# One block for the network and the second attention: the first sequence goes ahead beside the second sequence's down projection

## The reference

```python
x = x + _L0_attn_ref(_layernorm(x), wq, wk, wv, wo)            # 32 heads of 128, 8 key/value heads
x = x + _L0_ffn_ref(_layernorm(x), gate_t, up_t, down_t, ...)  # 512 -> 1792 -> 512, ternary weights with scales
x = x + _L1_attn_ref(_layernorm(x), w_qkv, b_qkv, w_out, b_out)# 32 heads of 16, ALiBi, causal
x = x + _L1_ffn_ref(_layernorm(x), A, B, Wr)                   # 64 experts, 16 picked
```

## Time and profile before

| what | value |
|---|---|
| median of 3 runs | 1610.68 us |
| the profiled execution's own time | 1609.08 us |
| its span | 1607.2 us |
| mean granted TensorE clock | 0.968 of full |
| share of the span: PE / DVE / ACT / POOL | 91 / 63 / 53 / 33 % |

### The profile page before, as it was taken

The page is one execution under the profiler, slowest core; times in us unless marked ns, Lnnn a source line. Parts: engine busy times, 40 slices in busy tenths (PEclk is TensorE's granted clock), DMA queues, the critical chain, the costliest instruction groups (busy, mean ns, idle before and its releaser), DMA issues. The chain is left out here.

```text
span 1607.2 us, 25387 instructions
## 1 busy us (share of the span) xinstructions
PE 1469.5 (91%) x7696; PEld 1208.1 (75%) x7696; DVE 1013.9 (63%) x2543; ACT 857.9 (53%) x2181; POOL 534.8 (33%) x465
## 2 busy tenths in 40 slices
PE   5999999999999999999778999995879999986798
PEld 3778888888888888888666888873667777764587
DVE  6676767676666676666544333344768888897543
ACT  2666555665566565556514233202768888894210
POOL 3673555545456554462400000005331313110500
PEclk9999999999999999999998999997889999997899
DMA  4010010101001010000002111005333444422000
GB/s 147 20 47 14 27 40 20 39 13 33 26 26 33 13 33 26 26 7 8 20 6 100 59 59 59 0 0 129 74 73 83 86 78 90 74 42 98 17 21 27
DMA packets 37468, 71.97 MB, mean 45 GB/s; under 512 B 4976, under 2 KB 5360, under 8 KB 36848
## 3 DMA queue, kind: packets, MB, share of 16 engines
q1 hardware_dynamic: 29664, 55.35, 11.3%
q0 software_dynamic: 7728, 15.73, 6.0%
HBM read 60.58 MB, written 10.49 MB: 44 GB/s over the span
## 5 line engine op out<-in xcount | busy, mean ns | idle before, releaser
L728 ACT ACTIVATE a_probs<-a_probs,a_least 128x512 f32<-128x512 f32 (+3 forms) x256 | 142.9, 559 | 175.6 <-DVE a_least L629 168.3
L377 POOL TENSOR_TENSOR a_rotated<-a_by_cos,a_by_sin 128x512 f32<-128x512 f32 x80 | 103.4, 1292 | 248.3 <-DVE a_by_sin L652 246.2
L637 DVE TENSOR_TENSOR a_probsT_lo<-a_ps_turn,a_probsT_hi 128x512 fp32r<-128x512 f32 (+3 forms) x256 | 118.7, 485 | 71.2 <-ACT a_probsT_hi L736 69.7
L736 ACT CAST a_probsT_hi<-a_ps_turn 128x512 fp32r<-128x512 f32 (+3 forms) x256 | 101.3, 426 | 102.0 <-PE a_ps_turn L526 102.0
L1532 ACT ACTIVATE a_probs<-a_probs,a_least 128x128 f32<-128x128 f32 (+3 forms) x256 | 142.3, 561 | 12.5 <-DVE a_least L1435 9.7
L1435 DVE CUSTOM_DVE_ANT_0 a_probs<-a_ps_score,a_causal 128x128 f32<-128x128 f32 (+3 forms) x256 | 117.2, 486 | 40.8 <-PE a_ps_score L1323 31.0
L782 ACT ACTIVATE a_probs<-a_probs,a_inverse 128x128 f32<-128x128 f32 (+3 forms) x256 | 123.2, 553 | 8.7 <-DVE a_inverse L690 7.5
L64 PE MATMUL a_ps_out<-a_wo_hi,a_attended_hi 128*128 128x512 f32 x256 | 105.5, 412 | 17.8 <-POOL a_wo_lo L371 15.6
L629 DVE CUSTOM_DVE_ANT_0 a_probs<-a_ps_score,a_causal 128x512 f32<-128x512 f32 (+2 forms) x192 | 101.1, 551 | 28.8 <-PE a_ps_score L66 28.7
L387 POOL TENSOR_TENSOR a_query_lo<-a_rotated,a_query_hi 128x512 fp32r<-128x512 f32 x64 | 82.6, 1290 | 105.8 <-ACT a_query_hi L748 105.8
L1443 DVE TENSOR_TENSOR a_probsT_lo<-a_ps_turn,a_probsT_hi 128x384 fp32r<-128x384 f32 (+1 forms) x192 | 108.9, 595 | 2.7 <-ACT a_probsT_hi L1541 2.6
(11 more groups left out here) (250 smaller groups left out, 4205.6 us busy)
## 6 DMA issues: line engine op xcount, KB each, us to landing
a_raw<-in_wq SPq DMA_DIRECT2D x36, 256.0 KB, 2.6
a_raw<-in_wo SPq DMA_DIRECT2D x36, 256.0 KB, 2.7
a_stacked_q<-a_spill_q POOLq DMA_DIRECT2D x48, 128.0 KB, 5.0
a_stacked_k<-a_spill_k POOLq DMA_DIRECT2D x24, 256.0 KB, 4.6
f_raw<-in_gate SPq DMA_DIRECT2D x14, 256.0 KB, 2.8
f_raw<-in_up SPq DMA_DIRECT2D x14, 256.0 KB, 3.0
f_raw<-in_down SPq DMA_DIRECT2D x14, 256.0 KB, 3.5
a_raw<-in_wk SPq DMA_DIRECT2D x12, 256.0 KB, 2.7
```

Of the source, the lines that this page charges most:

```text
L377: nc.gpsimd.tensor_tensor(rotated[:], by_cos[:], by_sin[:], ALU.add).then_inc(rotation_added, 1)
L637: nc.vector.tensor_tensor(probsT[1][:, t % 2, 0:w], ps_turn[:, t % 2, 0:w], probsT[0][:, t % 2, 0:w].bitcast(F32), ALU.subtract).then_inc( ...
L728: nc.scalar.activation(tile, tile, ACT.Exp, bias=least[:, slot, i:i + 1], scale=-1.0, accum_out=total[:, slot, i:i + 1]).then_inc(exp_done, 1)
L736: nc.scalar.copy(probsT[0][:, t % 2, 0:w], ps_turn[:, t % 2, 0:w]).then_inc(turned_hi, 1)
```

## The change

Both phases become one function with one block (`ffn0_attention1_phase`); the network is a class `Ffn0` whose parts are called by the engines' streams of the joint block. All its tiles and those of the attention lie at fixed places in one piece of SBUF and share the space as it comes free: `stacked_q` of a sequence lies on down-projection chunks 0 to 1 (2 to 3), `stacked_k` on 4 (5). PE tells of freed chunks by `chunk_free`.

The layer norm of the third layer has two parts of four tiles each, with the steps as methods. The PSUM banks are shared: the second sequence's down projection now goes to the four banks of gate and up, not to those of the first sequence.

```diff
@@ LayerNorm
+    def tiles(self, part): ...     # the tiles of one of `parts` parts
+    def shift / invert / normalise / split / root / round / turn / ready (…, part or tile)
@@ network, down projection of the second sequence
-            for t in range(QT):
-                at = slice(t * P, (t + 1) * P)
-                pe.wait_ge(out_scaled, t + 1)
-                for f in range(FC):
-                    mm = product(nc, ps_out[:, t, :], ...
+    def second_sequence(self, pe, t, chunks):
+        for f in chunks:
+            mm = product(nc, self.out_bank(t), ...
+            if f == FC - 1: mm.then_inc(self.out_done, 1)
+            elif t == NT - 1: mm.then_inc(self.chunk_free, 1)
@@ block.tensor
-            norm.tensor(pe)
-            pe.wait_ge(pick_in, 16)
+            ffn.tensor(pe)
+            ffn.second_sequence(pe, 4, range(FC))
+            ffn.second_sequence(pe, 5, range(half))
+            norm.turn(pe, 0)
+            ffn.second_sequence(pe, 5, range(half, FC))
+            norm.ready(pe, 0)
+            side_work(-1, 7)
+            ffn.second_sequence(pe, 6, range(half))
+            side_work(-1, 8)
+            ffn.second_sequence(pe, 7, range(half))
+            ffn.second_sequence(pe, 6, range(half, FC))
+            ffn.second_sequence(pe, 7, range(half, FC))
+            side_work(-1, 9)
...
+            pe.wait_ge(pick_in[0], 16)
+            pe.wait_ge(ffn.out_scaled, 6)
+            step(-1, 13)
+            side_work(-1, 10)
+            norm.turn(pe, 1)
+            pe.wait_ge(pick_in[1], 16)
             each_chunk(pe, step)      # now starts at step (-1, 14)
@@ block.vector
-            norm.vector(dve)
-            dve.wait_ge(consts_in, 16 * 3)
+            ffn.vector(dve)
+            for t in range(QT): ffn.add_out(dve, t)
+            norm.shift(dve, 0); norm.invert(dve, 0); normalise and split tiles 0 to 3
+            norm.normal_free(dve, 0)
+            ffn.add_out(dve, 4); ffn.add_out(dve, 5)
+            dve.wait_ge(bias_in, 16)
+            step(-1, 8); step(-1, 9)
+            ffn.add_out(dve, 6); ffn.add_out(dve, 7)
+            norm.shift(dve, 1)
+            dve.wait_ge(causal_in, 16)
+            step(-1, 13)
+            norm.invert(dve, 1); normalise tiles 4 to 7
+            step(-1, 11)
+            split tiles 4 to 7; norm.normal_free(dve, 1)
@@ block.scalar
-            norm.scalar(act)
+            ffn.scalar(act); norm.root(act, 0); norm.round(act, 0)
+            step(-1, 8); step(-1, 9); norm.root(act, 1)
+            step(-1, 10); step(-1, 11); norm.round(act, 1)
@@ block.sync
+            ffn.sync(sp)
+            sp.dma_start(bias[:], dram["bias1"]).then_inc(bias_in, 16)
+            sp.wait_ge(ffn.weights_split, 3 * FC)
             (wq, wk, wv, causal, wo)
+            write_out(-1, 7)
+            write_out(-1, 8)
+            sp.wait_ge(ffn.chunk_free, 8)
+            (out_bias)
+            write_out(-1, 15)
@@ block.gpsimd
+            def prepare(b):
+                pool.wait_ge(ffn.chunk_free, 2 * b + 2)
+                (half of `pick` for sequence b; clear stacked_q of b)
+            pool.wait_ge(ffn.made, 2 * FC)
             for what in ("wq", "wk", "wv"): split(1, ...)
-            (clear stacked_q) ; read_back(-1, 7), (-1, 8), (-1, 15) ; add the output bias ; chunk(0)
+            prepare(0)
+            read_back(pool, -1, 7)
+            pool.wait_ge(ffn.chunk_free, 5)
+            read_back(pool, -1, 8)
+            prepare(1)
+            read_back(pool, -1, 15)
+            chunk(0): read_back(pool, 0, 0), then add_out_bias(), then the split of wq
```

More of the change, by code:

```diff
@@ L141, in tensor, with turn @@
+    def scalar(self, act):
+        self.root(act, 0)
+        self.round(act, 0)
+    def turn(self, pe, part):
         nc, m, tiles_before = self.nc, self.m, self.tiles_before
@@ L144, in tensor @@
             pe.wait_ge(m.ident_in, 16)
-        for t in range(NT):
+        for t in self.tiles(part):
             pe.wait_ge(normal_done, tiles_before + t + 1)
@@ L839, in ffn0_phase @@
[L839 to L855, removed]
-                    sp.dma_start(raw[:, k, w, :], dram[name][f]).then_inc(raw_in[k][w], 16)
-            fetch(0, 0)
-            fetch(1, 1)
-            with sp.Fori(1, FC // 2) as i:
-                for k in range(2):
-                    fetch(2 * i + k, k)
@@ new lines, in scalar, with vector, copy_columns, split_lo @@
+        self.norm.scalar(act)
+        split_hi(0, 0, 1)
+        chunk(0, 0, 1)
+        chunk(1, 1, 1)
+        with act.Fori(1, FC // 2 - 1) as i:
+            for k in range(2):
+                chunk(2 * i + k, k, i + 1)
+        chunk(FC - 2, 0, FC // 2)
+        chunk(FC - 1, 1, FC // 2, last=True)
+    def vector(self, dve):
+        nc, gate, up, down = self.nc, self.gate, self.up, self.down
+        def copy_columns(f, k):
+            if isinstance(f, int) and f == 0:
+                dve.wait_ge(self.scales_in, 48)
+            wait(dve, self.hidden_made, 2 * f - 2)
+            nc.vector.tensor_copy(self.gate_col[:, k:k + 1], self.gate_s[:, bass.ds(f, 1)])
+            nc.vector.tensor_copy(self.up_col[:, k:k + 1], self.up_s[:, bass.ds(f, 1)]).then_inc(self.columns_copied, 1)
+        def split_lo(f, k):
@@ new lines, in add_to_sums @@
+                if last:
+                    mm.then_inc(self.out_done, 1)
+                elif t == QT - 1:
+                    mm.then_inc(self.summed, 1)
+        self.norm.tensor(pe)
+        make(0, 0, 0)
+        make(0, 0, 1)
+        make(1, 1, 0)
+        add_to_sums(0, 0, first=True)
+        make(1, 1, 1)
+        with pe.Fori(1, FC // 2) as i:
+            for k in range(2):
+                make(2 * i + k, k, 0)
+                add_to_sums(2 * i + k - 1, 1 - k)
+                make(2 * i + k, k, 1)
@@ L1405, in _ @@
         def _(dve):
-            norm.vector(dve)
-            dve.wait_ge(consts_in, 16 * 3)
+            ffn.vector(dve)
+            for t in range(QT):
+                ffn.add_out(dve, t)
+            norm.shift(dve, 0)
+            norm.invert(dve, 0)
+            for t in range(QT):
+                norm.normalise(dve, t)
+            for t in range(QT):
+                norm.split(dve, t)
+            norm.normal_free(dve, 0)
+            ffn.add_out(dve, 4)
+            ffn.add_out(dve, 5)
+            dve.wait_ge(bias_in, 16)
             def add_bias(c, s):
@@ L1517, in step @@
                     split_turned(*turning, 2)
+            step(-1, 8)
+            step(-1, 9)
+            ffn.add_out(dve, 6)
+            ffn.add_out(dve, 7)
+            norm.shift(dve, 1)
+            dve.wait_ge(causal_in, 16)
+            step(-1, 13)
+            norm.invert(dve, 1)
+            for t in range(QT, NT):
+                norm.normalise(dve, t)
+            step(-1, 11)
+            for t in range(QT, NT):
+                norm.split(dve, t)
+            norm.normal_free(dve, 1)
             each_chunk(dve, step)
@@ L1586, in step @@
                     round_operand(c1, s1)
+            step(-1, 8)
+            step(-1, 9)
+            norm.root(act, 1)
+            step(-1, 10)
+            step(-1, 11)
+            norm.round(act, 1)
             each_chunk(act, step)
```

563 lines of the change are left out of this document (304 added, 259 removed).

## The result

| | before | after |
|---|---|---|
| median (runs; lowest to highest) | 1610.85 us (4; 1609.86 to 1612.18) | 1585.90 us (4; 1583.85 to 1587.34) |
| the profiled execution's own time | 1609.08 us | 1584.94 us |
| its span | 1607.2 us | 1582.7 us |
| mean granted TensorE clock | 0.968 | 0.977 |

A forecast was written before the change was run, and what follows sets the result against it. PE, busy 91% of the span, was taken to lose time at the seam of the two phases and waiting for the second sequence's keys. 24.7 + 8.5 = 33.2 us gained gave 1577.5, stated as 1577, range 1571 to 1588.

The forecast's parts named there:

- Part 1: PE's stream from the second sequence's down projection to the first score: each inserted piece ready, values end at 1097.4.
- rival D: Down projection: inserted pieces not ready starve PE, 13 us per wait, three such waits about 1615; chance 0.04.
- Rival E: Joint block costs the network's loop what the seam gives, 2.4 us on each of 14 chunks; chance 0.02.
- Part 2: Keys' way through DRAM: issues end at 1090.8, landing 5.0 us later at 1095.8, first score at 1097.5.
- Rival C: Before the first score, POOL's chain chunk_free, clear, query, keys is the bound: loss 3 to 8 us; chance 0.15.
- Part 3: First score to first turn, second sequence's layer norm between: first turn at 1108.3 against 1133.0, 24.7 us earlier.
- Part 4: POOL's order for the second sequence's keys, read-back ahead of bias adds: 8.5 us gained, bounds 9.3 and 3.
- rival B: Second sequence's keys land late or wait for the output bias, the 8.2 us stay: loss 3 to 8; chance 0.17.

The follow-up runs named there:

- experiment 4: Changed kernel with pick's second half and the output bias issued only after the first keys have landed: 1585.24 us, ratio 0.9846.
- experiment 5: On top of experiment 4, POOL issues the keys' read-back only once all of the query has landed: 1587.61 us, ratio 0.9869.
- experiment 1: Changed kernel with POOL's old order: bias adds and split of wq again ahead of the second sequence's keys: 1588.80 us, ratio 0.9861.
- experiment 2: Changed kernel with each of POOL's bias adds waiting for the one before it, order kept: 1581.37 us, ratio 0.9814.
- experiment 3: Changed kernel with the bias adds moved ahead of the read-back of the second sequence's query: 1579.75 us, ratio 0.9808.
- experiment 7: Kernel before, phases apart, with only the second sequence's keys read back ahead of POOL's bias adds: 1604.96 us, ratio 0.9975.
- experiment 9: Changed kernel with bias adds early, pick's second half and output bias late, and stacked_q's down-projection chunks first for the last two tiles: 1574.56 us, ratio 0.9757.
- experiment 8: Kernel before with the bias adds ahead of the second sequence's query read-back, keys' read-back after the split of wq: 1604.07 us, ratio 0.9977.

## Why the prediction was right in kind and a third too high

The range held although two parts failed: together they cost 7.7 us of the 11 that it left above the forecast.

**Part 1 held.** PE stands nowhere between 1047.74 and the values' end, clock 1.00; 1096.08 against 1097.4. Each inserted piece was ready, and rival D (starved PE, slower) never began. The stretch took 48.34 us, all of them busy, where 49.6 were forecast. Rival E (the network's loop pays for it) fell too: the last hidden values end at 1047.68, before at 1047.63.

**Part 2 failed, by 2.4 us at the first score.** The step that failed is "issues end at 1090.8, landing 5.0 us later at 1095.8". The issues ended 0.8 us after it; the landing took 8.24. I had read the 5.0 from a place where query and keys were issued 3.6 us apart with nothing else behind the earlier trace rows; the query had landed 1.05 us after the first of the keys' issues. Now 0.87 us lie between them, and the query lands only 4.35 us after the keys' first issue. Besides, the bias (128x512, 0.25 MB) goes out just ahead of the keys and half of `pick` (32 partitions x 4096 values, 0.5 MB) just behind. Experiments 4 and 5 take the excess apart: 1.1 to 2.1 us of it from these two, 1.9 from the query. The prediction had named both transfers and left the sum at 5.0. Rival C ("POOL's chain is the bound") was right about the place, with 3.77 us of PE idle, but POOL was nearly on time; the transfers were not. The lower clock that it foretold came too (0.60 and 0.72 of full in the two windows after the gap).

**Part 3 was near.** First score to first turn was forecast at 10.8 us and took 11.66. Masks, four normalisations, four rests, table load and exponentials lie in the order that I summed. What is missing lies in ACT's last rounding, which ended 7.9 us after the first score, not 6.7; table load and exponentials then took 3.7, not 4.1. With part 2 the first turn came 21.5 us earlier, where 24.7 were forecast: 3.2 short.

**Part 4 failed by 4.5 us.** Its first half held: the read-back stood ahead of the adds and the wait fell from 8.14 to 1.05 (forecast 0.7), so rival B (these keys land late) was not it. What failed is the sentence that what is pushed back on POOL "ends at about 1176 as before and is wanted by side work of step 7 and later". It priced the adds by who waits for their results, and never asked what runs beside them. Eight adds with both operands in SBUF, back to back, now lay over a DVE multiply whose operands are both in SBUF; before, they had ended when it came. Experiments 1, 2, 3 and 7 show this: gone without the new order, gone with gaps, gone with the adds elsewhere, there without the joint block. DVE's operations with an operand in PSUM kept their times beside the same adds: a mask of 128x384 (L1530) took 0.55 us at 1140.81, in the middle of them, and 0.56 at 1101.33, with POOL idle. Stretch by stretch, 17.66 fell to 13.65 (4.0 won) and falls to 8.86 without the collision (8.8).

The Trainium skill has the rule: "SBUF — State Buffer", section "Who interferes with whom", says that only the port pair that DVE and GpSimd share brings contention, and the section on SBUF's two separate sides that it is an exclusive lock for a whole instruction, taken also by a DVE operation with two SBUF inputs against a GpSimd operation that reads SBUF. The traces agree on which operations collide; that it is a port that they share is the skill's account, and no run here shows it. I had weighed that page for DVE holding up POOL's descriptors, which no row here shows, and not for POOL holding up DVE, which makes the multiply 5.0 us longer here (5.47 against 0.42). By the Trainium skill's "SBUF — State Buffer", section "Summary: rules for kernel authors", the loser waits until the first instruction finishes, one add of 1.24 us at most; in the trace it waits until POOL's first gap at 1148.51, 5.2 us. Where the two differ, the trace decides.

One reading of the rows was wrong, though nothing in the sum hung on it. The six query issues at 1149.58 did not lie beside a busy DVE: it worked for 1.27 of the 2.99 us, and for 0.48 of the 3.07 us at 1114.14. The two rows don't compare a busy with an idle DVE.

**The balance.** In the profiled executions, 3.2 us are missing at the seam and 4.5 at the keys; that would leave 25.5. A further 2.1 us are lost in the attention's third chunk, where the keys' wait is 2.3 us instead of 1.5 with a granted clock of 0.78 instead of 1.00 after it, and 1.3 come back behind the last exponentials; the spans differ by 24.5. Such losses come and go between profiles: the second one of the changed kernel has 2.4 us in the second chunk and 1.8 in the third, the kernel before with the order alone 3.6 and 0.9. What makes these waits vary isn't settled. Without the two failed steps (experiment 9) the time is 1574.6, 38 us below the kernel before in the same set of runs, so the 33 us were there to be had, and a little more.

Not tried: splitting the clearing of `stacked_q` between engines.

## What to carry to other kernels

When a long run of POOL instructions is moved, ask not only who waits for its results but which DVE instructions with two SBUF operands will lie beside it. Put it where DVE works from PSUM, or leave a short gap between its instructions. And a landing time read at one spacing of transfers holds for that spacing only: when two read-backs move together, count what is still in flight when the second is issued. Work inserted into a dense stream of PE costs nothing but its own matmuls, if each piece is ready when PE reaches it.

## What the runs showed of the hardware that I had not expected

- The multiply did not wait for one POOL instruction but for the first gap in a row of them. Adds of 1.24 us each, back to back, held it through the rest of one, three more and the weight rounding behind them (5.47, 5.51, 5.58 and 5.40 us in four profiles, 4.47 in the kernel before with the order alone). Gaps of 0.08 us between the adds were enough for it to pass in 1.08 us.
- At its shortest the multiply takes 0.42 us (experiment 8). In the other twelve of the thirteen profiles, where it takes 0.59 to 5.58 us, it ends 0.28 to 0.29 us after a POOL instruction behind which there is a gap of 0.08 us or the issue of a transfer (1148.51 and 1148.80 in the changed kernel, 1145.53 and 1145.81 with the gaps).
- The keys' read-back (four transfers of 256 KB, the slopes among them) lands 4.8 us after its last issue when the query has landed before it is issued, and 6.6 to 6.8 when it is issued 0.9 to 1.0 us behind the query's 768 KB.
